# Layer 0's feed-forward network: W1 multiplied into the input weights, and VectorE takes the bias and maximum of every second chunk

## The reference, cut to what matters

```
s   = einsum('btd,dm->btm', x, Win) + bin_          # 64 values a row
h   = relu(s[..., None] * W1 + b1)                  # 64 x 16 = 1024 values a row
g   = einsum('btmh,mh->btm', h, W2) + b2
out = einsum('btm,md->btd', g, Wout) + bout
```

## Time and profile before

| | |
|---|---|
| median of 3 runs | 1029.87 us |
| profiled execution | 1030.26 us |
| its span, first to last instruction | 1028.4 us |
| mean granted TensorE clock | 0.967 of full |
| TensorE busy | 887.1 us, 86% |
| VectorE busy | 684.8 us, 67% |
| ScalarE busy | 473.2 us, 46% |
| GpSimd busy | 119.3 us, 12% |
| F0's chunk activation on ScalarE (line 989) | 32 of 775 ns mean |

### The profile page before, as it was taken

One profiled execution on the slowest core, in us unless ns is written; L12 is line 12 of the kernel. 1 busy time (PEld: TensorE's weight loads), 2 busy tenths in 40 slices (PEclk: granted clock), 3 DMA queues, 4 the chain that ended last, 5 costly groups with the idle time before them and its releaser, 6 DMA issues.

```text
span 1028.4 us, 14302 instructions
## 1 busy us (share of the span) xinstructions
PE 887.1 (86%) x4731; PEld 597.1 (58%) x4731; DVE 684.8 (67%) x2069; ACT 473.2 (46%) x1134; POOL 119.3 (12%) x206
## 2 busy tenths in 40 slices
PE   2688999978778779779999999999999988989965
PEld 1345445433334556656677676767667666777744
DVE  3835626292765977976768678668756677777744
ACT  0375564677676565565263442443243233322312
POOL 3000100040220310310001001001000111110102
PEclk9999999988979999999999999999999999999988
DMA  6700000000000000000000000000000000000000
GB/s 177 242 1 0 2 0 2 1 0 1 0 1 1 1 1 1 1 2 1 1 1 2 1 1 1 1 1 2 1 1 1 1 1 11 1 11 1 2 10 11
DMA packets 12063, 12.70 MB, mean 12 GB/s; under 512 B 3758, under 2 KB 7896, under 8 KB 11992
## 3 DMA queue, kind: packets, MB, share of 16 engines
q1 hardware_dynamic: 9272, 9.98, 3.2%
q10 hardware_dynamic: 2336, 1.29, 0.5%
q0 software_dynamic: 384, 0.53, 0.2%
HBM read 10.75 MB, written 1.05 MB: 11 GB/s over the span
## 4 chain that ended last, share of the span: by engine, by line
PE 60%; DVE 23%; ACT 7%; issue 5%; POOL 2%; ACTq 0%; POOLq 0%; DVEq 0%
PE bank L1679 10%; PE bank L1667 6%; PE bank L1669 5%; PE bank L1668 5%; PE bank L1587 5%; PE bank L1600 4%; DVE nm L1187 3%; PE bank L1472 3%; DVE hb L1331 3%; DVE hb L1322 2%; ACT PTs L962 2%; PE bank L1644 2%; PE bank L1425 2%; PE bank L1650 2%; PE bank L1725 2%
## 5 line engine op out<-in xcount | busy, mean ns | idle before, releaser
L999 ACT ACTIVATE hb<-bank 96x512 f32<-96x512 f32 (+1 forms) x160 | 95.1, 594 | 208.5 <-PE bank L1669 208.0
L1679 PEld LDWEIGHTS bank<-m_w,hb 128*128 128x128 f32 (+1 forms) x1280 | 166.6, 195 | 23.2 <-issue 5.5
L1667 PE MATMUL bank<-parts,m_w_lo 128*96 128x512 f32 (+1 forms) x320 | 152.5, 477 | 31.1 <-DVE hb L1322 22.6
L1679 PE MATMUL bank<-m_w,hb 128*128 128x128 f32 (+1 forms) x1280 | 176.3, 282 | 2.3 <-DVE hb L1322 2.1
L1331 DVE SCALAR_TENSOR_TENSOR hb<-hb,bank 96x512 f32<-96x512 f32 (+1 forms) x160 | 109.0, 681 | 93.4 <-ACT hb L999 92.5
L1669 PE MATMUL bank<-parts,m_w_hi 128*96 128x512 f32 (+1 forms) x320 | 127.8, 399 | 0.0
L1668 PE MATMUL bank<-parts,m_w_hi 128*96 128x512 f32 (+1 forms) x320 | 127.4, 398 | 0.0
L1322 DVE TENSOR_TENSOR hb<-hb,bank 96x512 f32<-96x512 f32 (+1 forms) x160 | 109.8, 686 | 10.4 <-PE bank L1669 4.9
L1667 PEld LDWEIGHTS bank<-parts,m_w_lo 128*96 128x96 f32 (+1 forms) x320 | 59.4, 186 | 78.0 <-DVE hb L1322 34.1
L1600 PE MATMUL bank<-Qs,KT 112*77 112x512 f32 x192 | 93.7, 515 | 11.1 <-ACT PTs L962 8.9
L1484 PE MATMUL bank<-KT,Qs 96*128 96x308 f32 x192 | 77.5, 428 | 13.4 <-ACT PTs L908 8.0
(11 more groups left out here) (271 smaller groups left out, 1502.3 us busy)
## 6 DMA issues: line engine op xcount, KB each, us to landing
m_w_raw<-in_L_ffn_w_dram SPq DMA_DIRECT2D x2, 1024.0 KB, 6.6
m_w<-in_L_ffn_W_dram SPq DMA_DIRECT2D x1, 1408.0 KB, 9.5
x<-in_x_dram ACTq DMA_DIRECT2D x4, 256.0 KB, 6.4
out_dram<-x SPq DMA_DIRECT2D x4, 256.0 KB, 2.0
f_out<-in_L_ffn_Wout_dram POOLq DMA_DIRECT2D x8, 64.0 KB, 3.5
m_w_raw<-in_L_ffn_W_experts_dram SPq DMA_DIRECT2D x1, 512.0 KB, 11.0
ctxn<-in_ctx_dram ACTq DMA_DIRECT2D x4, 38.5 KB
Wq<-in_L_xattn_Wq_dram SPq DMA_DIRECT2D x2, 64.0 KB
```

The source lines that it names most:

```text
L999: act.activation(hb[n % 3][0:m, :], bank[UP[u, n]][0:m, :], ACT.Tanh, scale=0.5).then_inc(*chunk_act.up(u, n))
L1667: pe.matmul(dst, w_lo, x_hi, start=True, stop=False)
L1679: op = pe.matmul(bank[7][:, t * P:(t + 1) * P], hb[n % 3][0:m, t * P:(t + 1) * P], wd, start=i == 0 and t == 0, stop=ends_expert(k, n) and ...
```

## The change

A new tensor `f0_w1` takes a broadcast of W1 to all 128 partitions (128 x 1024 values), and a product in place of the copy makes `f0_in` = Win * W1, so the chunk's relu needs no scale. Even chunks stay on ScalarE with a bias alone; odd chunks are done by VectorE as max(s + bias, 0), signalled by a new semaphore `chunk_max`. TensorE waits for the one or the other.

```diff
+            f0_w1 = tmp("f0_w1", [P, M0, I0])
...
+                act.dma_start(f0_w1[:].rearrange("p m i -> p (m i)"), a["L0_ffn_W1"].rearrange("m i -> (m i)").partition_broadcast(P)) \
+                    .then_inc(*landed["f0_w1"].up("all", by=16))
                 act.dma_start(graw[:, 0, :], a["g_xattn"].partition_broadcast(P)).then_inc(*landed["gates"].up(by=16))
...
-                dve.tensor_copy(f0_in[:].rearrange("p (m i) -> p m i", i=I0), nat_in[:].unsqueeze(2).to_broadcast([P, M0, I0]))
+                dve.wait_ge(*landed["f0_w1"].at("all"))
+                dve.tensor_tensor(f0_in[:].rearrange("p (m i) -> p m i", i=I0), f0_w1[:], nat_in[:].unsqueeze(2).to_broadcast([P, M0, I0]),
+                                  ALU.mult)
...
                     for c in range(C0):
                         yield
-                        act.wait_ge(*chunk_psum.at(u, c))
-                        room_in(c)
-                        act.activation(hb[c % 3], bank[TURN[c % 2]][:], ACT.Relu, scale=f0_cols[:, 0, c:c + 1],
-                                       bias=f0_cols[:, 1, c:c + 1]).then_inc(*chunk_act.up(u, c))
+                        if c % 2 == 0:
+                            act.wait_ge(*chunk_psum.at(u, c))
+                            room_in(c)
+                            act.activation(hb[c % 3], bank[TURN[c % 2]][:], ACT.Relu, bias=f0_cols[:, 1, c:c + 1]) \
+                                .then_inc(*chunk_act.up(u, c))
                         yield
...
                 if k == "F0":
-                    for _ in range(steps_body(k)):
-                        yield
+                    for c in range(C0):
+                        yield
+                        if c % 2:
+                            dve.wait_ge(*chunk_psum.at(u, c))
+                            if c >= 3:
+                                dve.wait_ge(*ffn_psum.at(u, c - 3))
+                            elif u[1]:
+                                dve.wait_ge(*last_use(("F", u[1] - 1)))
+                            dve.tensor_scalar(hb[c % 3], bank[TURN[c % 2]][:], f0_cols[:, 1, c:c + 1], 0.0, ALU.add, ALU.max) \
+                                .then_inc(*chunk_max.up(u, c))
+                        yield
+                    yield
+                    yield
...
-                        pe.wait_ge(*chunk_act.at(u, c))
+                        pe.wait_ge(*(chunk_max if c % 2 else chunk_act).at(u, c))
...
-                        reader[d] = (chunk_act, u, c)
+                        reader[d] = (chunk_max if c % 2 else chunk_act, u, c)
```

More of the change, by code:

```diff
@@ L258, in build @@
             landed = {n: sig("landed_" + n) for n in ("small", "side", "gates", "turn", "late_turn", "m2_w1", "m2_w2", "m2_w3", "m3", "m1_w1", "m1_w3",
-                                                      "rest", "mask", "f0", "rows")}
+                                                      "rest", "mask", "f0", "f0_w1", "rows")}
             zeroed = sig("zeroed")
@@ L609, in main @@
     rows_weighed, rows_paired, rows_summed = (sig(n) for n in "rows_weighed rows_paired rows_summed".split())
+    chunk_max = sig("chunk_max")
     (chunk_psum, chunk_act, chunk_silu, chunk_ready, ffn_psum,
```

## The result

| | before | after |
|---|---|---|
| median (8 runs each, taken together) | 1029.41 us | 1033.38 us |
| lowest to highest | 1024.37 to 1031.05 | 1031.11 to 1037.45 |
| profiled execution, its span | 1030.26, 1028.4 | 1031.11, 1029.4 |
| mean granted clock in it | 0.967 | 0.968 |

The medians differ by 4.0 us. The ratio of the runs is 1.005, with an interval of 1.0031 to 1.007, which is 5 us, between 3.2 and 7.2. I had said 1031.0, +0.7, in a range of 1027 to 1036.

What follows compares the result with a forecast made beforehand. TensorE was taken as the bound beside layer 0's attention, VectorE in A1's preparation, ScalarE and TensorE in turn among A1's heads. +0.3 + 0.4 + 0.4 - 0.4 = +0.7 on 1030.26 gave 1031.0 us, range 1027 to 1036.

Steps and rivals of the forecast that it cites:

- Prices: Operation times: ScalarE's bias-only chunk 0.68 us, VectorE's chunk 0.65 (0.60 in a full queue, bounds 0.4 to 0.75), product 1.2.
- The factor of three: Skill rule that VectorE does relu up to three times faster, making the chunk some 0.25 us; the prediction sided against it.
- Prologue: Weight loading before the units: VectorE's lateness hidden under its 2.79 us wait, a later `side` adding 0.3 us.
- My bound of 2.1: Upper bound in us on the prologue's loss through a later `side`; 0.3 was taken, lower bound 0.
- Beside layer 0: Two F0 units beside layer 0's attention: chunk 1 +0.3, chunk 4 -0.1, so +0.2 us each, +0.4 together.
- the gaps absorb 0.64: Among layer 0's score blocks, VectorE's idle gaps of 0.25 and 0.39 us take up chunk 1; cost +0.3, bounds 0 and 0.65.
- The 0.1 that I gave back for chunk 4: Beside layer 0, chunk 4 stays on ScalarE, 0.1 us shorter between two exponentials for which TensorE waits: -0.1.
- First A1 unit: First F0 unit beside A1: `feat` 1.8 us later, `hid` +1.2, chunk 6 -0.1, chunk 7 -0.67; sum +0.4.
- the margin of 0.6: First A1 unit: slack in us between the end of `feat`'s product and `hid`, used up first by VectorE's lateness.
- Second A1 unit: Second F0 unit beside A1: +0.4 us by ScalarE's own chain, chunk 6 -0.1, chunk 7 -0.67; sum -0.4.
- The margin of 1.65: Second A1 unit: slack in us before `hid`, leaving only +0.2 of `feat`'s lateness.
- VectorE's queue pays in full: Rival: each chunk ahead of `feat` or layer 0's last maximum costs its whole 0.75 us; +5.7, 1036.0; chance 0.15.

Runs made afterwards that it cites:

- the versions with two operations: Before's weights and loads, VectorE takes chunks 6 and 7, or 7 alone, as scale-and-bias then maximum: 1026.22 and 1026.6 us; 1026.52 with 7 alone.

## Why the prediction was off, step by step

The time fell into the range, and the way was right. But the sum of +0.7 was far too small: three of its terms were too low, and the fourth swings from profile to profile. The range held only because it had been drawn out to the rival's price.

**Prices: right for two, low for one.** ScalarE's chunk 0.68 as said, the product 1.22 for 1.2. VectorE's chunk: said 0.65 (0.60 of a full queue), measured 0.747 (0.67 of the queue: 127.41 to 128.08). The upper row, the 0.749 operation with two sources, was the right neighbour.

One page bears on that size. The Trainium skill's "VectorE: DVE Perf Modes", section "The TRN2 errata", has in its table 120 cycles and one an element for an operand in PSUM at 0.96 GHz, an estimate of 0.66 us for this chunk; the rows of 0.747 disagree by 0.09, and the measurement decides. The factor of three that the prediction took from the Trainium skill's "ScalarE: Activation LUTs", section "Rules for kernel authors", is stated there for bf16; this chunk is fp32, and VectorE's 0.747 is longer than ScalarE's 0.682.

**Prologue: said +0.3, measured +1.04.** That VectorE's later `small` would be hidden held: its line starts 1.52 later (18.39 to 19.91) and it still waits for TensorE:

```profile
21.52 1.22 DVE L433 TENSOR_TENSOR f_in<-f_w,nat_in 128x1024 f32<-128x1024 f32 x1
22.66 1.65 DVE L438 TENSOR_SCALAR f_out<-f_out,f_cols 128x128 f32<-128x128 f32 x8
...
22.67 0.55 PE L492 MATMUL bank<-f_b,f_wout 64*128 64x1 f32 x2 [6.66 <-DMA m_b<-in_L_ffn_b_experts_dram]
...
26.09 0.16 DVE L440 TENSOR_TENSOR f_bias<-bank,f_bout 128x1 f32<-128x1 f32 x1 [1.79 <-PE bank L496]
```

The wait is 1.79 for 2.79. What failed is the sentence that SP issues `side` after the engines have gone quiet, and so unmoved. That was a misreading, since SP issues `side` from 12.6 to 19 us and only its later part into quiet engines. And I took an issue's time as fixed; it isn't. SP's queue, before and then after (start, us):

```profile
7.47 0.43 SPq L305 DMA_DIRECT2D Wq<-in_L_xattn_Wq_dram  x1
7.94 0.58 SPq L305 DMA_DIRECT2D Wk<-in_L_xattn_Wk_dram  x1
...
18.95 0.27 SPq L320 DMA_DIRECT2D m_b<-in_L_ffn_b_experts_dram  x1
```

```profile
7.48 1.58 SPq L306 DMA_DIRECT2D Wq<-in_L_xattn_Wq_dram  x1
9.10 0.98 SPq L306 DMA_DIRECT2D Wk<-in_L_xattn_Wk_dram  x1
...
20.51 0.27 SPq L321 DMA_DIRECT2D m_b<-in_L_ffn_b_experts_dram  x1
```

With 512 KB more issued on ScalarE's queue at 5 us, the same issues on SP take 1.58 and 0.98 us for 0.43 and 0.58, and every later one follows 1.6 late. The first of them took 1.58 to 2.69 us in all five profiles with the early load and 0.43 in all nine without; an issue on ScalarE's own queue beside it took 1.23 instead of 0.35. It is not that the DMA engines are full just then: their share from 7.4 to 9.1 us is 0.69, before 0.66, and from 12 to 16 us, at a share of 1.10, issues take no longer than in before. What holds the issues back is open. TensorE's wait for `side` ends 1.05 later (21.62 to 22.67), and the block with it. My bound of 2.1 held it; I chose from the wrong end. Kernels with the early load lost 0.64 to 1.22 here, with the late one 0.00 to 0.76, and with none -0.70 to 0.51, so the scatter of the prologue is as large as the term. The Trainium skill's "DMA: Bandwidth & Descriptors", section "Rules for kernel authors", says that spreading loads over the issuing engines brings no bandwidth, as they share 16 DMA engines, and only saves issue time; the rows fit the sharing, and show that a load on one queue can lengthen the issues on another.

**Beside layer 0: said +0.2 a unit, measured 0.65.** The failed step is "the gaps absorb 0.64". VectorE's idle gaps there were not room but the rhythm in which it and TensorE hand banks to each other; an operation ahead of the whole run moves both engines and leaves the gaps as they are. Moving the load (0.65, 0.68), doubling the operation (1.24, 1.27), no VectorE chunk (0.00), and a chunk inside the run (0.16, 0.20) all fit. The upper bound of chunk 1, 0.65, is what it cost. Chunk 3 at 0 was right: with chunk 1's 0.65 of queue nothing is left for it. The 0.1 that I gave back for chunk 4 is not seen: with every activation shorter and no VectorE chunk the two units stay at 0.00.

**First A1 unit: said +0.4, measured +2.57.** The work ahead of `feat` was nearly right: within the unit the copy of the transposed maxima is 1.30 later, and the product of `feat` starts 1.95 later (237.72 to 243.14, less the 3.47 from before the unit), said 1.8. `hid` follows 1.67 later, said 1.2. What failed is behind it. ScalarE's rows, as the earlier trace rows:

```profile
239.45 2.03 ACT L922 ACTIVATE Qs<-bank 16x512 fp32r<-16x512 f32 x4 [1.48 <-PE bank L1519]
241.50 1.28 ACT L925 ACT_TABLE_LOAD   x1
243.97 0.27 ACT L925 ACTIVATE hid<-bank,t_b 64x16 f32<-64x16 f32 x1 [1.19 <-PE bank L1528]
246.30 0.27 ACT L928 ACTIVATE hid<-bank,t_b 64x16 f32<-64x16 f32 x1 [2.06 <-PE bank L1533]
```

As said, the table load no longer matters: `hid` waits 1.19 for TensorE behind `feat`. Its 1.67 is the 1.95 of `feat` and 0.30 more for the product of `feat` (0.79 for 0.49), less the margin of 0.6. But from the first to the second `hid` are 2.33 us, before 0.71. TensorE between them:

```profile
243.14 0.79 PE L1528 MATMUL bank<-feat,t_w1b 128*64 128x16 f32 x6 [1.73 <-DVE feat L1239]
243.87 2.08 PE L1668 MATMUL bank<-xff,f_in 128*128 128x512 f32 x2
245.87 0.39 PE L1533 MATMUL bank<-hid,t_w2T 64*64 64x16 f32 x2
```

Chunk 6's product stands in TensorE's order between the two small products of the temperature. Before it took 1.12 us there; now, at 1.2 GHz after a wait of 1.73, it takes 2.08, and the second small product and `hid` wait behind it. That makes the step 1.62 longer; I had named the clock beside the rival only. But most of it is not the change's. Before's second profile has the slow product too, after a shorter wait:

```profile
238.70 0.79 PE L1510 MATMUL bank<-feat,t_w1b 128*64 128x16 f32 x6 [1.07 <-DVE feat L1232]
239.42 2.08 PE L1650 MATMUL bank<-xff,f_in 128*128 128x512 f32 x2
```

There the step is 2.05. Of the six variants that add nothing to VectorE's preparation four have 2.05 to 2.15 and two 0.78 and 0.81, while the variant with the even chunks on VectorE has 1.00 and the doubled operation 1.39. In before's second profile the stretch behind the step gave 0.78 of it back. Against that profile the first A1 unit costs 2.04 and not 2.57.

The other piece is chunk 7. Copies as the earlier trace rows:

```profile
254.30 0.60 ACT L868 ACTIVATE Os<-bank 128x512 f32<-128x512 f32 x1 [0.92 <-PE bank L1605]
...
258.83 0.60 ACT L868 ACTIVATE Os<-bank 128x512 f32<-128x512 f32 x1 [0.92 <-PE bank L1605]
...
262.80 0.60 ACT L868 ACTIVATE Os<-bank 128x512 f32<-128x512 f32 x1 [0.90 <-PE bank L1605]
```

The group takes 4.53 for 4.64, so 0.11 for 0.67. It is 4.51 to 4.54 in all ten profiles without chunk 7 on ScalarE, but also 4.55 and 4.54 in the two where ScalarE has it with a bias alone, so even the 0.11 is mostly the shorter activation. TensorE still has the chunk's product and its share of the output in that group, and its products are what the copies wait for; I had named it, and given it no price. The steps from the second `hid` to the first copy are 0.62 shorter (8.00 for 8.62), which gives part back: 1.67 + 1.62 - 0.62 - 0.11 = 2.56.

**Second A1 unit: said -0.4, measured -1.02**, and in other profiles of after and its neighbours +0.39, +0.56 and +0.31. Its group with chunk 7 takes 4.09 for 4.63 (315.47 to 319.56), so here chunk 7 does give 0.54. The same group takes 4.08 to 4.10 in all ten profiles without chunk 7 on ScalarE and 4.55 to 4.63 in the four with it; why it gives so much more here than in the first unit is open. The margin of 1.65 took `feat`'s lateness, as forecast: `hid` starts 0.02 later within the unit (0.16 in the second profile), said 0.4. The remaining -0.50 of after's -1.02 lies between `hid` and the first copy and swings with the clock, so the sign of the unit is not settled.

**Sum.** Said 0.3 + 0.4 + 0.4 - 0.4. Measured 1.04 + 1.33 + 2.57 - 1.02 = 3.9 without the scatter before F0. The medians' +4.0 agrees, the ratio's +5 is above it. The measured sum lies two thirds of the way to the rival "VectorE's queue pays in full" (+5.7), to which I gave 0.15. It had the place right, but not the count: it charged three chunks beside layer 0 (2.2), where the one ahead of the maxima in each unit cost 1.33 in all, and 4.5 beside A1, where `feat` came 1.95 later in the first unit and the second's margin took its share.

## What to carry over

An idle gap of an engine is room for an operation that stands close to it (here one maximum ahead of the gap); ahead of the whole run in which two engines hand buffers to each other it was paid in full, so price it there by its queue time. A load added to one queue early in a kernel can hold up the issues on another: look for the path's own small loads behind it. Issuing the load last got back 0.3 of 1.0; moving the small loads ahead of it was not tried. And an operation moved off an engine brings only the distance to the engine that is late next: price that engine's own work in the same group first.

## What the runs showed of the hardware

**The same wait, two clocks.** From 697 us on all kernels have the same instructions, yet the rest took 331.2 us in before, 328.8 in after and 326.5 to 327.0 in eight of the other profiles, after's second among them. Before's second profile and two of the variants have 331.3 (the load with all chunks on ScalarE, and the doubled operation), the one with the even chunks 329.8. TensorE, in before, after a wait of 1.32 us:

```profile
764.96 0.58 PE L1667 MATMUL bank<-parts,m_w_lo 128*128 128x512 f32 x1 [1.32 <-DVE lg L1110]
765.34 0.63 PE L1668 MATMUL bank<-parts,m_w_hi 128*128 128x512 f32 x1
```

and in the kernel with chunk 7 alone on VectorE (late load), after the same wait:

```profile
764.49 0.50 PE L1685 MATMUL bank<-parts,m_w_lo 128*128 128x512 f32 x1 [1.32 <-DVE lg L1117]
764.83 0.40 PE L1686 MATMUL bank<-parts,m_w_hi 128*128 128x512 f32 x1
```

One runs on at 1.2 GHz (granted clock 0.54 from 764.96 to 768 us), the other at 2.4 (1.00), and the dip costs about 1.5 us. Behind 697 us before has three such places that the profiles with 326.5 to 327.0 lack, near 765, 799 and 884 us, some 4.6 us in all. Before's runs spread over 6.7 us, from 1024.4 to 1031.1; three such dips would make most of that, though only its profiled runs show them. Which dips a kernel falls into, and whether its edit shifts the odds, no run here settles. The gain of the versions with two operations may be nothing else: in their profiles the rest took 326.5 and 326.6.

**A DMA issue has no fixed time.** One issue on SP took 0.43 us in nine profiles, and 1.58 to 2.69 us at the same place in the five where a load of 512 KB more had been issued early on another engine's queue.
